# Issuing the first loads of Wk and x from ScalarE instead of SyncE

## What is computed

```
x: (2, 1024, 256)   ctx_1024: (2, 154, 256)   16 heads of 64, 16 experts of 64 slots
def xattn(xn, ctx):
    q = xn @ Wq + bq;  k = ctx @ Wk + bk;  v = ctx @ Wv + bv          # 256 -> 1024
    s = where(mask, -1e30, q k^T / 8);  return softmax(s) v @ Wo + bo
def ffn(x):
    x = layernorm(x, norm_g, norm_b);  se = layernorm(slot_embeds, slot_g, slot_b) * scale
    logits = einsum('bnd,esd->bnes', x, se)
    dispatch = softmax(logits, over n);  combine = softmax(logits, over e and s)
    slots = einsum('bnd,bnes->besd', x, dispatch)
    eout = (gelu(slots @ Wg + bg) * (slots @ Wu + bu)) @ Wd + bd
    return einsum('bns,bso->bno', combine, eout)
x = x + xattn(layernorm(x), ctx_1024)
x = x + ffn(layernorm(x))
```

## Time and profile before

| | us |
|---|---|
| median of 3 runs | 544.42 |
| lowest and highest run | 544.23, 544.68 |
| the profiled execution, its own time | 544.24 |
| the profiled execution, its span | 542.5 |
| TensorE busy in the span | 530.0 |
| VectorE, ScalarE, GpSimd busy | 434.1, 402.2, 303.3 |

### The profile page before, as it was taken

The page is one execution under the profiler, slowest core; times in us unless marked ns, Lnnn a source line. Parts: engine busy times, 40 slices in busy tenths (PEclk is TensorE's granted clock), DMA queues, the critical chain, the costliest instruction groups (busy, mean ns, idle before and its releaser), DMA issues.

```text
span 542.5 us, 11967 instructions
## 1 busy us (share of the span) xinstructions
PE 530.0 (98%) x3896; PEld 499.8 (92%) x3896; DVE 434.1 (80%) x1305; ACT 402.2 (74%) x1098; POOL 303.3 (56%) x327
## 2 busy tenths in 40 slices
PE   6999999999999999999998999999999999999997
PEld 4889999999999999999997888999978888899997
DVE  6777878787897979899677998798699888865453
ACT  5879969596896959779564555788979889766562
POOL 6674654544545455454365768787467999910000
DMA  8635000000030000000001333150288888525551
GB/s 257 181 86 179 3 1 2 2 2 1 3 98 2 2 2 1 2 0 4 0 1 80 155 156 156 78 201 1 79 264 283 270 306 288 182 79 170 181 167 67
DMA packets 34901, 54.11 MB, mean 100 GB/s; under 512 B 3997, under 2 KB 21497, under 8 KB 34713
## 3 DMA queue, kind: packets, MB, share of 16 engines
q1 hardware_dynamic: 34841, 53.36, 29.7%
HBM read 40.54 MB, written 10.49 MB: 94 GB/s over the span
## 4 chain that ended last, share of the span: by engine, by line
PE 90%; ACT 4%; DMA 2%; POOL 1%; DVE 1%; issue 1%; SPq 0%; ACTq 0%; DVEq 0%
PE ps L1461 9%; PE ps L1585 9%; PE ps L1357 9%; PE ps L1369 8%; PE ps L1610 8%; PE ps L1499 8%; PE ps L1439 7%; PE ps L1552 7%; PE ps L1476 5%; PE ps L1632 4%; PE ps L1501 4%; PE ps L1644 3%; DMA wvo_raw<-in_L_xattn_Wo_dram 2%; ACT expo L885 1%; PE ps L1615 1%; PE ps L1622 1%
## 5 line engine op out<-in xcount | busy, mean ns | idle before, releaser
L885 ACT ACTIVATE expo<-expo,nmin 128x154 f32<-128x154 f32 x256 | 106.2, 423 | 5.3 <-DVE nmin L1135 4.8
L1135 DVE CUSTOM_DVE_ANT_0 expo<-ps,maskb 128x154 f32<-128x154 f32 x256 | 69.1, 312 | 11.9 <-PE ps L1461 11.9
L723 POOL TENSOR_TENSOR prob_t<-expo,prec 128x104 f32<-128x104 f32 x64 | 23.1, 360 | 89.3 <-DVE prec L1146 89.1
L726 POOL TENSOR_TENSOR prob<-expo,prec 128x512 f32<-128x512 f32 x64 | 66.8, 1043 | 0.0
L1461 PE MATMUL ps<-kbd,qT_high 128*128 128x308 f32 x256 | 61.1, 323 | 0.0
L1155 DVE TENSOR_TENSOR pT_low<-ps,pT_high 128x512 fp32r<-128x512 f32 (+1 forms) x96 | 57.2, 596 | 4.1 <-ACT pT_high L899 3.9
L788 POOL TENSOR_TENSOR w_gu_low<-w_raw,w_gu_high 128x1024 fp32r<-128x1024 f32 x17 | 50.3, 2966 | 16.2 <-ACT w_gu_high L835 16.1
L899 ACT CAST pT_high<-ps 128x512 fp32r<-128x512 f32 (+1 forms) x96 | 49.1, 513 | 10.8 <-PE ps L1476 8.1
L803 ACT ACTIVATE oT_high<-ps,bqv_c 128x256 fp32r<-128x256 f32 x64 | 29.8, 466 | 34.8 <-PE ps L1501 34.7
L885 ACT ACTIVATION_READ_ACCUMULATOR expo<-expo,nmin 128x1 f32 x256 | 50.3, 196 | 0.0
L1461 PEld LDWEIGHTS ps<-kbd,qT_high 128*128 128x128 f32 x256 | 39.8, 190 | 0.2
(11 more groups left out here) (241 smaller groups left out, 1762.7 us busy)
## 6 DMA issues: line engine op xcount, KB each, us to landing
logits_dram<-lsb SPq DMA_DIRECT2D x16, 512.0 KB, 2.6
w_raw<-in_L_ffn_Wg_dram SPq DMA_DIRECT2D x16, 512.0 KB, 4.0
w_raw<-in_L_ffn_Wu_dram SPq DMA_DIRECT2D x16, 512.0 KB, 4.5
w_raw<-in_L_ffn_Wd_dram SPq DMA_DIRECT2D x16, 512.0 KB, 4.5
lraw<-logits_dram SPq DMA_DIRECT2D x13, 512.0 KB, 3.8
out_dram<-gate SPq DMA_DIRECT2D x16, 128.0 KB, 2.2
kbd<-keys SPq DMA_DIRECT2D x12, 154.0 KB, 2.8
wvo_raw<-in_L_xattn_Wv_dram SPq DMA_DIRECT2D x2, 512.0 KB, 7.0
```

Source lines behind the costliest of these rows:

```text
L726: pool.tensor_tensor(prob[:, n % 2, :, heads, :], expo[:, n % 2, pp, :, :, 0:P], prec[:, n % 2, pp].unsqueeze(3).to_broadcast([P, 2, 2, P] ...
L885: ins = act.activation(row, row, ACT.Exp, scale=-1.0, bias=nmin[:, n % 2, pp, j, h:h + 1], accum_out=psums[:, n % 2, pp, j, h:h + 1])
L1135: ins = dve.tensor_tensor_reduce(out=expo[:, n % 2, pp, j, h, :], in0=ps[:, s % NS, h * SK:(h + 1) * SK], in1=maskb[:, (2 * (n // QUADS) + ...
```

## The change

`("x",)` and `("split", WK, 0)` leave `LOADS`, and with them SyncE's list. The same two transfers, to the same places and with the same semaphores, stand at the head of ScalarE's list, Wk first, ahead of the wait for `const_pool` and of the fill of `vt`. No wait is added or taken away, and no computing instruction moves.

```
 LOADS = [
-    ("x",), ("split", WK, 0), ("split", WQ, 0), ("bias",), ("split", WK, 1), ("split", WV, 1),
+    ("split", WQ, 0), ("bias",), ("split", WK, 1), ("split", WV, 1),
     ("split", WK, 2), ("split", WV, 0), ("mask",), ("split", WQ, 1), ("split", WQ, 2),
 ]
...
-            elif ev[0] == "x":
-                sp.dma_start(x1[:, 0:2], x_t[:, 0, 0:2]).then_inc(d_x, 16)
...
+        lo, hi = PIECES[WK][0]
+        act.dma_start(weight_half(WK, 0)[2], Wk.rearrange("(k p) n -> p k n", p=P)[:, :, lo:hi]).then_inc(d_w[WK][0], 16)
+        act.dma_start(x1[:, 0:2], x.rearrange("b (p t) d -> p b t d", p=P)[:, 0, 0:2]).then_inc(d_x, 16)
         act.wait_ge(const_pool, 1)
```

## The result

| | before | after |
|---|---|---|
| median, us | 544.68 (543.62 to 545.21, 11 runs) | 545.70 (545.07 to 546.39, 11 runs) |
| ratio | | 1.0022, 95% interval 1.0013 to 1.0032 |
| the profiled execution, its own time and its span | 544.24, 542.5 | 545.55, 543.7 |

The change makes the kernel slower by 0.22% or 1.2 us by the ratio. In a second series beside later experiments the ratio was 1.0026 (1.0016 to 1.0037). The time forecast, 545.2, is half a microsecond low and the range holds the result. Half of that comes from the base: the forecast was added to a median of 544.42, and over all runs that of before is 544.68, so that the medians differ by 1.0 us. The loss itself is beyond doubt; that it is over 0.2% is not, for the interval spans that bound.

The account below looks back on a forecast made before the run. The prediction took TensorE's chain, whose head waits for ctx, to bound the kernel. Terms 0 + 0 + 0 + 0.8 us on 544.24 gave 545.0, or 545.2 us from the median 544.42; range 544.2 to 546.1.

Parts of the forecast that it names:

- What bounds the kernel, and that nobody waits for the moved loads: Kernel's head: TensorE, 90% of the chain, waits for ctx; Wk has 0.5 us to spare, earlier x gains 0.
- SyncE's queue: Loads behind the two moved issues go out about 0.87 us earlier, the bias among them; gain 0.
- ScalarE's own issues: Start of ScalarE: two added issues, 0.87 us, covered by 1.47 us idle before cT_high; cost 0.
- ctx's landing: Start of the chain: Wk and x pass beside ctx and delay it by 0.8 us, bounds 0 and 1.1.
- x's share: In ctx's delay: x passing beside ctx_tail's 53 KB, 0.16 us by equal bytes or 0.31 by equal rows.
- the interleaved end: Loading of ctx: full interleaving of Wk and x with it costs 0.93 to 1.08 us.
- Rival B: At ctx's loading: ctx unharmed, served first or Wk passing in the early low rate; 544.4, up to 544.8; chance 0.23.
- Rival C: ctx_tail pushed beyond about 4.7 into the slow stretch: +1.4 to +1.55, 545.8 to 546.0; chance 0.19.
- Rival D: At K 0 and K 1: faster through an earlier 2.4 GHz clock, about 543.0; chance 0.06.
- Rival E: At the seven warm-ups before K 3: TensorE's clock rises later, +1.4 on top of 0.8, 546.6; chance 0.06.
- From ctx to the end one to one: Chain from 4.02 us to the end: every step shifts whole with ctx; possible 0.25 us back from the clock taken as 0.
- The chances: Whole kernel, beyond 0.2% (1.09 us) or not: same 0.69, slower 0.25, faster 0.06.

## Why the prediction was right, and where it was not

- **What bounds the kernel, and that nobody waits for the moved loads: right, in one direction.** Neither Wk nor x is on the chain after. A later x is another matter: with x landing at 6.99 the kernel was 0.29% slower.
- **SyncE's queue: right in the trace shown**, the bias follows ctx directly and K 0 doesn't move for it. The second trace of before shows that the bias can be last; there the earlier issue would be worth the few hundredths of a microsecond by which K 0 was late.
- **ScalarE's own issues: right.** Forecast 0.87 us and vt ready at 4.8; measured 0.99 (0.48 + 0.51, with gaps 1.05) and 5.00. Hidden.
- **ctx's landing: the right mechanism, its size too small.** Forecast +0.8, with 1.1 as the upper bound; measured +1.21 and +1.23. The bytes themselves were priced right: 0.75 measured against 0.77, where Wk stood ahead of ctx on one queue. Three parts of the term were off. The credit of 0.14 us, for Wk passing in spare time between 1.80 and 2.40, wasn't there: no row of ScalarE's queue passed before 2.44 in either trace of after. x's share was put at 53 KB in the sum; by 4.50 us 0.12 to 0.15 MB of x had passed (0.38 and 0.41 less Wk's 0.26). With that, ctx's last packet is 1.08 and 1.03 us later, which is the interleaved end of 0.93 to 1.08. The sum had nothing for the last part: the landing follows this packet by 0.73 us and not by 0.60, and why is open. The agreement of the interleaved sum with the packets is in part luck, since the sum goes by 340 GB/s throughout, and up to 3.60 us one trace of after has 0.13 MB less than before and the other none less. By the rule of the Trainium skill, "DMA: Bandwidth & Descriptors", section "Queues, rings and completion order", that each engine takes turns between queues with work, the sum was the interleaved end. The traces agree in part: from 2.4 to 2.7 us on, rows of Wk and of ctx pass side by side, but with x alone 0.19 MB of x passed up to 3.00 us beside 0.03 MB of ctx.
- **Rival B fell** (ctx served first): 4.02 became 5.22. **Rival C fell** by its own mark: the slow stretch of 86 GB/s is gone, 365 stand in its place. Yet the landing at 5.18 is nearly as late as it said, and for a similar reason: in the first trace, between 3.60 and 4.40, SyncE's queue got only 0.08 MB, the end of ctx, of the engines' 0.31. **Rival D** did not come. **Rival E** came in part: in the first trace the step fell into the seven warm-ups and K 3 was 1.43 us late with ctx 1.21. But the step's lateness also shows without the change and is gone in the second trace of it, so nothing shows it to be a cost of the change.
- **From ctx to the end one to one: right for the head, blurred behind it.** SyncE's first store of logits comes at the end of attention. Its row in the traces of before and of Wk alone on ScalarE:

```profile
292.83 49.39 SPq L625 DMA_DIRECT2D logits_dram<-lsb  x16
```

```profile
293.15 49.41 SPq L625 DMA_DIRECT2D logits_dram<-lsb  x16
```

K 3 was 1.16 us late in the second, the logits only 0.32, and its span was 542.7 us; yet its 12 runs have a median of 545.69, and this execution is the fastest of them. In the two traces of the change the same row starts at 294.16 and 294.55, 1.33 and 1.36 us behind the first and the second trace of before. So there the delay of ctx arrives whole, and between 16 and 293 us single executions gain or lose up to 0.8 us against each other. This is why spans of single traces are not used as results here. What in attention does it is open, and so is why the loss is 1.2 us where Wk stood ahead of ctx on one queue and ctx was only 0.75 us late.
- **The chances.** Most of the weight was on no change beyond 0.2%, 1.09 us. The loss is 1.2 us. With the term at its interleaved end, 0.93 to 1.08, the forecast would have stood just below that bound, and the weight of "slower" should have been about a half.

## What to carry to other kernels

Before a load is moved to a second queue, look for the transfer that the chain waits for, and count what would pass beside it, or even ahead of it. Here a load of 0.32 MB landed 1.2 us later, because 0.38 to 0.41 MB of a second queue passed by the time it was through. A transfer that nobody waits for gains nothing by an earlier issue and takes its bytes from the one that somebody does; put it behind, in the same queue. A load's slack has to be read on both sides, since the engine that uses it may have the chain's next step standing behind it.

## What was not expected

- The push of a second queue is not proportional: 0 for 4 KB, 0.66 us for 128 KB, 1.11 to 1.17 for 256 KB and 1.17 to 1.23 for 512 KB, against a load of 308 KB in the first queue.
- Of two queues whose loads are issued at the same instant, either can begin: SyncE's with Wk on the other queue (ctx from 1.85 us, Wk from 2.44 to 2.68), ScalarE's with x or half of x on it (x from 1.8, ctx from about 2.4).
- What passes from 2.40 to 3.60 us differs from trace to trace: 249 to 316 GB/s with two large loads on two queues, and 267 to 340 with the loads of before, where the engines reach 365 later on.
- The same issue of x takes 0.51 us on ScalarE where it took 0.35 on SyncE; but alone on ScalarE it takes 0.43, and on SyncE, with ctx_tail on ScalarE, 0.45. So it is not the issuing engine alone that sets it.
- Three warm-ups of 0.43 us in the standstill ahead of the keys went with a step from 1.2 to 2.4 GHz at 10.0 to 10.5 us instead of after 11.7, in both kernels that had only these three, one trace each; with three more ahead of ctx its transposes ran at 2.4 GHz, and the keys behind a standstill of 0.93 us at 1.2 again.
